# A recurrent and ternary feed-forward layer on eight cores: redundant waits leave the recurrence, one multiply goes from VectorE to ScalarE, and four steps of each output chunk go from VectorE to GpSimd

## What is computed

```
xn = layernorm(x)
# attention part: a recurrence over the sequence, state of 128
xB = xn @ B.T
state_t = tanh(state_{t-1} @ A.T + xB_t)
y  = states @ C.T + D*xn + xn
a  = layernorm(y) * gamma + beta
# feed-forward part: ternary weights with a scale per output row
h = silu((xn@w1.T)*s1) * ((xn@w2.T)*s2)       # 1024 -> 4096
h = gelu((h@h1.T)*h1s)                        # 4096 -> 4096
h = gelu((h@h2.T)*h2s)                        # 4096 -> 4096
out = x + a + (h@w3.T)*w3s                    # 4096 -> 1024
```

## Time and profile before

| what | value |
|---|---|
| median of 2 timed runs | 7627.12 us (7550.39 and 7703.85) |
| the profiled execution, its own time | 7251.64 us |
| its span, on the slowest core | 7250.1 us |
| spans of all cores | 7216.3 to 7250.1 us |
| mean granted TensorE clock of the cores | 0.947 to 0.950 |
| PE busy | 5312.8 us (73%) |
| DVE busy | 1430.1 us (20%) |
| ACT busy | 666.4 us (9%) |
| POOL busy | 91.8 us (1%), DMA issues only |
| DMA | 936.64 MB, mean 129 GB/s |

### The profile page before, as it was taken

One profiled execution on the slowest core, in us unless ns is written; L12 is line 12 of the kernel. 1 busy time (PEld: TensorE's weight loads), 2 busy tenths in 40 slices (PEclk: granted clock), 3 DMA queues, 4 the chain that ended last, 5 costly groups with the idle time before them and its releaser, 6 DMA issues.

```text
span 7250.1 us, 65114 instructions; the slowest of 8 cores (7216.3 to 7250.1 us)
## 1 busy us (share of the span) xinstructions
PE 5312.8 (73%) x24252; PEld 2439.2 (34%) x24252; DVE 1430.1 (20%) x2720; ACT 666.4 (9%) x1334; POOL 91.8 (1%) x169
## 2 busy tenths in 40 slices
PE   0421110299959995999589968996899689968996
PEld 0310000034423442344234423443344334433442
DVE  3411113730033003300240024002400240024002
ACT  0012210010001010100010001000100010001000
POOL 0000000000000000000000000000000000000000
PEclk9999999999979997999799979997999799989998
DMA  3299998234434443344334433443344334433442
GB/s 94 90 108 112 110 113 112 78 134 151 153 108 134 151 152 110 131 154 151 110 126 153 151 116 124 155 151 115 124 153 151 115 124 155 150 114 125 152 153 104
DMA packets 189720, 936.64 MB, mean 129 GB/s; under 512 B 21348, under 2 KB 22629, under 8 KB 112872
## 3 DMA queue, kind: packets, MB, share of 16 engines
q1 hardware_dynamic: 158872, 739.53, 28.8%
q0 software_dynamic: 25936, 176.17, 15.0%
q10 hardware_dynamic: 4608, 16.78, 0.8%
HBM read 1007.90 MB, written 109.05 MB: 154 GB/s over the span
## 4 chain that ended last, share of the span: by engine, by line
PE 67%; DVE 6%; DMA 5%; issue 2%; ACT 1%; SPq 0%; POOL 0%; DVEq 0%; POOLq 0%; ACTq 0%
PE pE L601 49%; PE pA L541 6%; PE pB L546 5%; PE pH L628 3%; PE pG L628 3%; DMA xrb<-x 2%; DMA l1ring<-w2b 2%; PE pA L484 1%; DVE xnbt L493 1%; DVE t1b L671 1%; DVE t1b L679 1%; DVE t1b L685 1%; DVE t2b L682 1%; DVE t2b L668 1%; DVE t2b L675 0%
## 5 line engine op out<-in xcount | busy, mean ns | idle before, releaser
L601 PE MATMUL pE<-hbuf,hring 128*128 128x512 bf16 x8192 | 1787.1, 381 | 30.7 <-DVE hbuf L572 28.8
L601 PE MATMUL pE<-g1buf,hring 128*128 128x512 bf16 x8192 | 1769.7, 379 | 8.1 <-ACT g1buf L608 7.4
L601 PEld LDWEIGHTS pE<-hbuf,hring 128*128 128x128 bf16 x8192 | 804.5, 98 | 1013.3 <-issue 60.6
L601 PEld LDWEIGHTS pE<-g1buf,hring 128*128 128x128 bf16 x8192 | 800.7, 98 | 977.0 <-issue 13.9
L636 DVE TENSOR_SCALAR ffn_fm<-pG,w3spk_s 128x512 f32<-128x512 f32 x32 | 24.0, 751 | 3781.7 <-PE pG L628 3781.7
L541 PE MATMUL pA<-xnbt,l1ring 128*128 128x512 bf16 x2048 | 499.2, 388 | 98.1 <-DMA l1ring<-w2b 47.0
L546 PE MATMUL pB<-xnbt,l1ring 128*128 128x512 bf16 x2048 | 488.5, 382 | 0.0
L392 PE MATMUL pE<-states,atb 128*128 128x8 bf16 x560 | 97.7, 174 | 523.2 <-ACT states L399 523.2
L554 ACT ACTIVATE thbuf<-pA,s1h 128x512 f32<-128x512 f32 x256 | 175.9, 687 | 1900.3 <-PE pB L546 1900.3
L608 ACT ACTIVATE g1buf<-pE,h1spk_s 128x512 bf16<-128x512 f32 x256 | 175.9, 687 | 1641.5 <-PE pE L601 1641.5
L608 ACT ACTIVATE hbuf<-pE,h2spk_s 128x512 bf16<-128x512 f32 x256 | 175.9, 687 | 1601.9 <-PE pE L601 1601.9
(11 more groups left out here) (80 smaller groups left out, 1864.7 us busy)
## 6 DMA issues: line engine op xcount, KB each, us to landing
hring<-h1b SPq DMA_DIRECT2D x256, 1024.0 KB, 5.1
hring<-h2b SPq DMA_DIRECT2D x256, 1024.0 KB, 4.9
xrb<-x POOLq DMA_DIRECT2D x128, 512.0 KB, 4.1
l1ring<-w1b SPq DMA_DIRECT2D x256, 256.0 KB, 2.6
l1ring<-w2b SPq DMA_DIRECT2D x256, 256.0 KB, 2.9
hring<-w3b SPq DMA_DIRECT2D x64, 1024.0 KB, 4.9
h1b<-h1t POOLq DMA_DIRECT2D x1, 32768.0 KB, 464.7
h2b<-h2t POOLq DMA_DIRECT2D x1, 32768.0 KB, 775.1
```

The source lines that it names most:

```text
L601: op("tensor", lambda e, p=pe_, s=hs, kk=k, r=rsrc: e.matmul(p[:, 0:512], hslot(s)[:, kk * 128:(kk + 1) * 128], r[:, kk * 512:(kk + 1) * 512],
```

## The change

1. In the recurrence two waits go: TensorE no longer waits for VectorE's add of the step before (`vsc`), and VectorE no longer waits for the tanh of two steps before (`ac`). Both are implied by the wait that stays.
2. In stage L1 the scaled product `ubuf` is made by ScalarE (an activation with Copy and a scale per partition), behind its tanh, and not by VectorE.
3. In the output stage the four VectorE steps L668, L679, L682 and L685 become GpSimd instructions, with a new semaphore `p7`. The chunk's steps then change engine four times: VectorE, GpSimd, VectorE, GpSimd, VectorE.
4. In the output stage the odd chunks are transposed into pG and pH, the even ones into pE and pE2.

```diff
@@ recurrence
             wait("tensor", ac, n)
-            if n >= 2:
-                wait("tensor", vsc, n - 1)
             mn = op("tensor", lambda e, bk=bank, off=63 + i: e.matmul(
                 bk[:, 0:8], atb[:], stv(off), start=True, stop=True), smm)
             wait("vector", smm, mn)
-            wait("vector", ac, n - 1)
@@ L1
                 gwait("scalar", ("th", m % 2))
+                gwait("scalar", "usilu_u")
                 thn = op("scalar", lambda e, p=pa, g=m, sl=m % 2: e.activation(
                     thbuf[:, sl * 512:(sl + 1) * 512], p[:, 0:512], AF.Tanh,
                     scale=s1h[:, g:g + 1]), scL)
-                wait("vector", mmL, mmL.n)
-                wait("vector", scL, thn)
+                un = op("scalar", lambda e, p=pa, g=m: e.activation(
+                    ubuf[:], p[:, 0:512], AF.Copy, scale=s1h2[:, g:g + 1]), scL)
+                gset(ka, (scL, un))
+                wait("vector", scL, un)
                 gwait("vector", "usilu")
                 if m == 0:
                     gwait("vector", "hbuf_w")
-                un = op("vector", lambda e, p=pa, g=m: e.tensor_scalar(
-                    ubuf[:], p[:, 0:512], s1h2[:, g:g + 1], None, op0=OP.mult), vL)
-                gset(ka, (scL, thn), (vL, un))
-                wait("vector", scL, thn)
-                wait("vector", vL, un)
                 sn = op("vector", lambda e, sl=m % 2: e.scalar_tensor_tensor(
                     silubuf[:], thbuf[:, sl * 512:(sl + 1) * 512], 1.0, ubuf[:],
                     op0=OP.add, op1=OP.mult), vL)
                 gset(("th", m % 2), (vL, sn))
+                gset("usilu_u", (vL, sn))
@@ output
+                pF, pF2 = (pE, pE2) if cloc % 2 == 0 else (pG, pH)
+                kF, kF2 = ("pE", "pE2") if cloc % 2 == 0 else ("pG", "pH")
...
-                wait("vector", v7, t1n)
-                t2n = op("vector", lambda e: e.tensor_tensor(
-                    t2b[:], t1b[:], d1b[:], op=OP.mult), v7)
-                wait("vector", v7, t2n)
+                wait("gpsimd", v7, t1n)
+                t2n = op("gpsimd", lambda e: e.tensor_tensor(
+                    t2b[:], t1b[:], d1b[:], op=OP.mult), p7)
+                wait("vector", p7, t2n)
...
-                gn = op("vector", lambda e: e.tensor_tensor(
-                    t1b[:], t2b[:], gbc[:], op=OP.mult), v7)
-                wait("vector", v7, gn)
+                wait("gpsimd", v7, ln_)
+                gn = op("gpsimd", lambda e: e.tensor_tensor(
+                    t1b[:], t2b[:], gbc[:], op=OP.mult), p7)
+                wait("gpsimd", p7, gn)
...
-                s1n = op("vector", lambda e, sl=slot: e.tensor_tensor(
-                    t1b[:], t2b[:], xrb4[:, sl * DM:(sl + 1) * DM], op=OP.add), v7)
-                gset(("xrb4", slot), (v7, s1n))
-                wait("vector", v7, s1n)
+                s1n = op("gpsimd", lambda e, sl=slot: e.tensor_tensor(
+                    t1b[:], t2b[:], xrb4[:, sl * DM:(sl + 1) * DM], op=OP.add), p7)
+                gset(("xrb4", slot), (p7, s1n))
+                wait("vector", p7, s1n)
...
-                    pE[:, 0:512], op=OP.add), v7)
-                gset("pE", (v7, o1n))
+                    p[:, 0:512], op=OP.add), v7)
+                gset(kF, (v7, o1n))
```

More of the change, by code:

```diff
@@ L136, in _build @@
                  "mmH", "scH", "mmW", "vW", "mmC2", "vC2", "mmT3",
-                 "v3", "x3", "x4", "mmF", "v7", "vout", "sout", "sdbg", "vsc")
+                 "v3", "x3", "x4", "mmF", "v7", "vout", "sout", "sdbg", "vsc", "p7")
         SM = {n: Sem(es.enter_context(nc.semaphore(n))) for n in names}
@@ L141, in _build @@
          sc2, v5b, wl, wlB, wh, mmL, scL, vL, mmH, scH, mmW, vW, mmC2,
-         vC2, mmT3, v3, x3, x4, mmF, v7, vout, sout, sdbg, vsc) = (
+         vC2, mmT3, v3, x3, x4, mmF, v7, vout, sout, sdbg, vsc, p7) = (
             SM[n] for n in names)
@@ L641, in _build @@
             gset("hbuf_w", (mmW, mmW.n))
-            for cloc in range(4 if p3sub >= 7 else 0):
+            for cloc in range(4):
                 c = 4 * tj + cloc
@@ L649, in _build @@
                 wait("tensor", vW, W3_END_VW)
-                gwait("tensor", "pE")
-                gwait("tensor", "pE2")
+                gwait("tensor", kF)
+                gwait("tensor", kF2)
                 for mo in range(8):
-                    bank = pE if mo < 4 else pE2
+                    bank = pF if mo < 4 else pF2
                     cc0 = (mo % 4) * 128
@@ L677, in _build @@
                     rstdy[:, cc:cc + 1], op0=OP.subtract, op1=OP.mult), v7)
-                wait("vector", v7, ln_)
-                gn = op("vector", lambda e: e.tensor_tensor(
-                    t1b[:], t2b[:], gbc[:], op=OP.mult), v7)
-                wait("vector", v7, gn)
-                an = op("vector", lambda e: e.tensor_tensor(
-                    t2b[:], t1b[:], bbc[:], op=OP.add), v7)
-                wait("vector", v7, an)
-                s1n = op("vector", lambda e, sl=slot: e.tensor_tensor(
-                    t1b[:], t2b[:], xrb4[:, sl * DM:(sl + 1) * DM], op=OP.add), v7)
-                gset(("xrb4", slot), (v7, s1n))
-                wait("vector", v7, s1n)
+                wait("gpsimd", v7, ln_)
+                gn = op("gpsimd", lambda e: e.tensor_tensor(
+                    t1b[:], t2b[:], gbc[:], op=OP.mult), p7)
+                wait("gpsimd", p7, gn)
+                an = op("gpsimd", lambda e: e.tensor_tensor(
+                    t2b[:], t1b[:], bbc[:], op=OP.add), p7)
+                wait("gpsimd", p7, an)
+                s1n = op("gpsimd", lambda e, sl=slot: e.tensor_tensor(
+                    t1b[:], t2b[:], xrb4[:, sl * DM:(sl + 1) * DM], op=OP.add), p7)
+                gset(("xrb4", slot), (p7, s1n))
+                wait("vector", p7, s1n)
                 gwait("vector", ("out", slot))
-                o1n = op("vector", lambda e, sl=slot: e.tensor_tensor(
+                o1n = op("vector", lambda e, sl=slot, p=pF: e.tensor_tensor(
                     out_sb[:, sl * DM:sl * DM + 512], t1b[:, 0:512],
-                    pE[:, 0:512], op=OP.add), v7)
-                gset("pE", (v7, o1n))
-                o2n = op("vector", lambda e, sl=slot: e.tensor_tensor(
+                    p[:, 0:512], op=OP.add), v7)
+                gset(kF, (v7, o1n))
+                o2n = op("vector", lambda e, sl=slot, p=pF2: e.tensor_tensor(
                     out_sb[:, sl * DM + 512:(sl + 1) * DM], t1b[:, 512:1024],
-                    pE2[:, 0:512], op=OP.add), vout)
-                gset("pE2", (vout, o2n))
+                    p[:, 0:512], op=OP.add), vout)
+                gset(kF2, (vout, o2n))
                 gset("t1t2", (v7, o1n), (vout, o2n))
```

## The result

The changed kernel is slower: its time is 1.016 times that of before, with a 95% interval of 1.010 to 1.022. The median of its 11 runs is 7797.94 us, that of 10 runs of before 7627.12. The profiled execution took 7368.93 us, 117 us more than that of before, and this is the difference that the views account for.

A forecast was written before the change was run, and what follows sets the result against it. TensorE held 67% of the span; in the output stage chunk, store and load ran without overlap. Output +182, recurrence -4 and L1 -8 gave +170 us on the median 7627.12: 7797 us, range 7400 to 7950.

The forecast's parts named there:

- Output, GpSimd's step: Output stage: each of four steps takes 2.30 us on GpSimd for VectorE's 1.225, 4.3 us more a chunk.
- Output, handoffs: Output stage: passing between engines adds 1.4 us a chunk, with 0.6 us taken for VectorE to GpSimd.
- Output, banks: Output stage: transposing odd chunks into pG and pH gains 0, since the load of x covers the transposes.
- Recurrence: Two waits fewer save 0.18 us a step, 100 us in all, but only 4 us net reach the second block.
- L1: Multiply on ScalarE shortens a block's chain by some 0.2 us; weight loads come nearly as late, so -8 us.
- GpSimd at VectorE's speed: Rival, output stage: steps of 1.225 us and handoffs of 0.10 add 0; 7615 us, not slower; chance 0.26.
- Upper end of GpSimd's cost: Rival, output stage: steps of 3.37 us and handoffs of 0.6 throughout; 7986 us, +4.7%; chance 0.12.
- The recurrence's 100 us in full: Rival, recurrence: the whole saving reaches the end, sum +74 us, 7701 us, +1%; chance 0.08.
- Table loads between tanh and Copy: Rival, L1: ScalarE changes its function table, 1.28 us a load, +328 us, 8125 us; chance 0.03.

The follow-up runs named there:

- the early loads: Each output chunk's x load issued one chunk earlier, against the kernel with eight slots and multiply moved (fourth edit also added): input and output stages 754.0 to 567.7 us.
- the deeper ring: The kernel before with eight slots for L1's weights instead of four: L1 falls from 1048 to 958.5 us.

## Why the prediction was right

The direction, the mechanism and the place of each term were right; the sum was 170 us for 119 measured, +2.2% for +1.6%. The measured ratio lies just inside 2%, to which the prediction had given 0.36, against 0.60 for slower by over 2%. That the predicted 7797 us meets the median of 7797.94 is luck: the single runs behind it lie between 7375 and 8049 us, and the sum itself was 51 us too high.

- Output, GpSimd's step: taken as 2.30 us, the middle of the bounds, measured 2.335. The reasoning by which it was reached (the columns count twice) fits the size; no run tested it as a cause.
- Output, handoffs: this is the term that was mis-sized. The 0.6 us from VectorE to GpSimd was read at DMA issues, and it belongs to those. For arithmetic it is 0.15, from GpSimd to VectorE no more than between VectorE's own steps and between GpSimd's own steps 0.14. Predicted 1.4 us a chunk for all handoffs, measured 0.16 (147.2 / 32 = 4.60 us a chunk in all, less 4 x 1.11 for the steps; 1.11 is 2.335 less 1.225). That is 40 us too much in all, and the steps were 5 us too low; the two small gains came out 17 us larger than predicted. Less half a microsecond that the other stages took more, this is the 51 by which the sum was too high.
- Output, banks: 0, right, and for the reason given, shown by taking the cover away.
- Recurrence: 0.18 us a step from one early step of the trace was right (the recurrence is 103 us shorter, 0.185 x 558). That nearly all of it vanishes under the conversions was right, and shown. The net was put at 4 us and is 9 to 14, in the changed kernel 9.0: the two more chunks were right, but the 9.6 us by which the conversions were to end later are 4.0 there. Why two loads of 0.52 MB cost them less than their bytes would take is not shown. The other 4.2 us of the second block's earlier start lie ahead of the recurrence and were in no term.
- L1: -8 predicted, about -15 measured. The chain became 0.29 us shorter, not 0.2, since ScalarE starts the multiply before the tanh is through. The cover by the weight loads was right in kind: it took half of the edit's worth.
- GpSimd at VectorE's speed: excluded by the 2.335 us. Upper end of GpSimd's cost: excluded likewise. The recurrence's 100 us in full: excluded. The Trainium skill (GPSIMD Engine Reference, 3.1 Elementwise) gives 4497 ns for 2048 columns; half of that, an estimate, is 2.25 us, and the 2.335 us measured for 1024 lie 4% above it.
- Table loads between tanh and Copy: none. The changed kernel has one on its tanh line, as before. This agrees with what the Trainium skill (ScalarE: Activation LUTs, section on table sets) states, that copy is in every set.

## What to carry to other kernels

Work moved to an idle engine helps only if it runs beside something. In a chain of steps on the same two buffers each step counts in full, and on the slower engine it costs the difference (here 1.11 us, 128 times).

Before an edit that shortens a chain, ask what stands right beside it: a transfer that ends at the same time hid some nine tenths of one edit here, half of another and all of a third. The order matters: the early loads and the deeper ring gave most (186 and 90 us), and only with them did the banks (55 us for 0) and the multiply (29 for 15) show their worth. And before a difference of a few us is put down to an edit, look where in time it arises: a third of the second block's earlier start arose ahead of the first edited line.

## What the runs showed of the hardware

- A wait that is already met is not free when it stands behind the one that decides: about 0.07 us on VectorE and 0.11 us on TensorE, 0.18 us in a step of 1.11. It is an instruction of its own: 1116 went with the 558 waits on each of the two engines.
- A 0.5 MB load issued by ScalarE's queue beside the large conversions takes about 49 us from chunk to chunk, alone 3.6 us to landing; the DMA engines are busy with a share of 0.98 to 1.01 all the while. With two such loads more the conversions took 852.6 us for 848.6.
- ScalarE starts an activation without a wait 0.58 us after one of 0.69 us, so two in a row cost 1.26 us.
- GpSimd's arithmetic starts 0.15 us after VectorE's step, its DMA issue 0.59 us. A VectorE step waits no longer for GpSimd's than for one of its own (0.10 us).
